# A buffer kept through the top-p steps: the mixing stage's first loads and its fold are moved into the end of the second step

## The reference

```python
# second layer, X = relu(norm(x))
for s in range(2):
    A = _adj_from_feats(Xa, W1, W2, W3)   # top-p softmax of Xa W1 W2 (Xa W3)^T
    Xf = R @ Xf
    Xa = A @ Xa
    Z = Z + (Xf @ U1s[s] + Xa @ U2s[s])
Y = X + Z
return (Y - mu) * rsqrt(var + LN_EPS) * gamma + beta
...
# third layer, 8 heads of 64
Wh = einsum('nf,hfd->hnd', x, W)
e_src = einsum('hnd,hd->hn', Wh, a1)
e_dst = einsum('hnd,hd->hn', Wh, a2)
```

## Time and profile before

| | |
|---|---|
| runs of the kernel | 3787.61, 3789.25, 3791.85 us |
| the profiled execution | 3794.3 us, span 3792.5 us |
| TensorE matmul, busy | 3378.6 us, 89% |
| VectorE, busy | 3207.5 us, 85% |
| ScalarE, busy | 2818.0 us, 74% |
| GpSimd, busy | 1394.7 us, 37% |
| DMA queue of SyncE (hardware) | 178.22 MB, 14.9% of 16 engines |
| second top-p step's last store | issued at 2320.5 us |
| mixing stage's first and last instruction | 2323.74 and 2486.6 us |

### The profile page before, as it was taken

One profiled execution on the slowest core, in us unless ns is written; L12 is line 12 of the kernel. 1 busy time (PEld: TensorE's weight loads), 2 busy tenths in 40 slices (PEclk: granted clock), 3 DMA queues, 4 the chain that ended last, 5 costly groups with the idle time before them and its releaser, 6 DMA issues. The chain is left out here.

```text
span 3792.5 us, 56639 instructions
## 1 busy us (share of the span) xinstructions
PE 3378.6 (89%) x20572; PEld 2050.0 (54%) x20628; DVE 3207.5 (85%) x5502; ACT 2818.0 (74%) x3508; POOL 1394.7 (37%) x1048
## 2 busy tenths in 40 slices
PE   7799999986969976899999965889999898999999
PEld 3699999743434433444444432368878443444444
DVE  3699999679999999599999996579998424999996
ACT  5699999559999999299999981267787334666664
POOL 0387444114545556146555661145553110000000
PEclk9999999998979988999999987999999999999999
DMA  6721110120111112311101004310000221111110
GB/s 235 270 79 31 36 31 25 57 67 26 53 37 36 46 44 97 117 47 45 34 20 28 25 17 130 147 26 21 21 21 10 74 77 67 48 48 55 51 50 17
DMA packets 166377, 224.46 MB, mean 59 GB/s; under 512 B 90466, under 2 KB 102720, under 8 KB 162976
## 3 DMA queue, kind: packets, MB, share of 16 engines
q1 hardware_dynamic: 147200, 178.22, 14.9%
q0 software_dynamic: 18896, 42.46, 3.5%
HBM read 148.36 MB, written 72.00 MB: 58 GB/s over the span
## 5 line engine op out<-in xcount | busy, mean ns | idle before, releaser
L1798 DVE SCALAR_TENSOR_TENSOR junk<-expd,mid 128x2048 bf16<-128x2048 f32 x440 | 1034.7, 2352 | 13.9
L604 ACT ACTIVATE steepz<-s1b,thr_h 128x512 bf16<-128x512 f32 (+1 forms) x928 | 774.3, 914 | 32.3 <-DVE A L675 20.3
L1694 ACT ACTIVATE junk_s<-expd,nmid 128x2048 bf16<-128x2048 f32 x250 | 498.5, 1994 | 3.8 <-POOL nmid L1736 3.4
L1698 ACT ACTIVATE junk_s<-junk_s 128x2048 bf16<-128x2048 bf16 x250 | 477.9, 1912 | 6.0
L758 PE MATMUL acc<-V,B 128*128 128x198 bf16 x4096 | 442.7, 251 | 35.3 <-DVE B L677 13.8
L765 PE MATMUL acc<-V,adjT 128*128 128x99 bf16 (+1 forms) x5248 | 415.5, 218 | 0.0
L1752 POOL TENSOR_SCALAR reach<-above,lack 128x1 f32<-128x1 f32 x202 | 231.5, 1146 | 457.8 <-ACT lack L1701 457.7
L1754 POOL TENSOR_SCALAR nmid<-reach,steps,nmid 128x1 f32<-128x1 f32 x202 | 377.5, 1869 | 21.2
L758 PEld LDWEIGHTS acc<-V,B 128*128 128x128 bf16 x4096 | 341.4, 98 | 38.6 <-issue 26.3
L765 PEld LDWEIGHTS acc<-V,adjT 128*128 128x128 bf16 x5248 | 340.4, 98 | 40.0 <-issue 0.3
L1553 PE MATMUL psX<-parts,block 128*128 128x512 bf16 x1482 | 339.1, 383 | 14.1 <-POOL ident L209 4.5
(11 more groups left out here) (319 smaller groups left out, 6230.5 us busy)
## 6 DMA issues: line engine op xcount, KB each, us to landing
rows<-in_adj_dram SPq DMA_DIRECT2D x16, 1024.0 KB, 8.7
s1b<-sT_dram SPq DMA_DIRECT2D x32, 512.0 KB, 3.7
block<-adj_dram SPq DMA_DIRECT2D x32, 512.0 KB, 4.4
plain_table<-rows POOLq DMA_DIRECT2D x16, 512.0 KB, 8.3
adj_dram<-adjT POOLq DMA_DIRECT2D x4, 2048.0 KB, 21.7
veil_table<-fill POOLq DMA_DIRECT2D x64, 128.0 KB, 2.5
y_dram<-yo SPq DMA_DIRECT2D x32, 256.0 KB, 2.0
adjT<-adj_dram SPq DMA_DIRECT2D x4, 2048.0 KB
```

Source lines behind the costliest of these rows:

```text
L604: act.activation(steepz[:, m % RELUS, :], s1b[:, q % 4, :], ACT.Relu, bias=thr_h[:, u, 1, j:j + 1], scale=STEEP).then_inc(relu_ready, 1)
L1694: act.activation(junk_s[:, u, :], expd[:, slot[i], :], ACT.Relu, bias=col(nmid, i), accum_out=col(above, i)).then_inc(sums_ready, 1)
L1698: act.activation(junk_s[:, u, :], junk_s[:, u, :], ACT.Sign, accum_out=col(over, i)).then_inc(sums_ready, 1)
L1798: link(dve.scalar_tensor_tensor(junk[:, :], e, col(mid, i), e, ALU.is_gt, ALU.mult, accum_out=found))
```

## The change

`adjT` is taken once, at the start of the program, and kept. While it holds no adjacency it serves as scratch: `xt`, `xo` and `rest` of `elu_project_stage`, and `expd`, `junk`, `junk_s` and `xo` of the top-p steps are views of it. So `parts` needn't be given back before the mixing stage, and the mixing stage's buffers `yt`, `xt`, `wp`, `gam`, `bet`, `avec` and `xo` are views of `parts` (class `Early`); its `w` is `w_out`, which held the keys `KT`. Since they exist in the step, a new letter `Z` in SyncE's string loads them there, once the last logits and the last `spread` are done: wp, avec, gam, bet, four tiles of xt, U2, and four tiles of yt. VectorE makes the eight pieces of the fold at the end of step 1. The mixing stage begins with tiles 4 and on, has no fold, and `BEHIND` is one less. The semaphores of the early loads belong to a scope of their own, which ends behind the mixing stage with one more clearing and barrier.

```diff
-         "giaagiyagiyaagiygiyagiyagiyagiyaagiyagiyagiyagiyagiygiygiygiyyxxxxx")},
+         "giaagiyagiyaagiygiyagiyagiyagiyaagiyagiyagiyagiyagiygiygiygiZyyxxxxx")},
...
+    def top_p_step(self, s, nat, tr, KT, w13n, parts, block16, xa_dram, xT_dram, kq_dram, parts_dram, y_dram,
+                   scratch, early, x_dram, w_dram, a1_dram, a2_dram):
...
-            expd = self.sb(st, "expd", [P, ROW_BLOCKS, N])
+            R = 2 * ROW_BLOCKS
+            expd = scratch[:, 0:R * N].bitcast(F32).rearrange("p (r n) -> p r n", r=ROW_BLOCKS)
+            junk = scratch[:, R * N:(R + 1) * N]
...
+                    elif c == "Z":
+                        sp.wait_ge(logits_ready, NT)
+                        sp.wait_ge(spread_ready, NT)
+                        for k in range(KD):
+                            sp.dma_start(early.wp[:, k, :].rearrange("p (h d) -> p h d", h=early.H),
+                                         w_dram[:, tile(k), :].rearrange("h p d -> p h d")).then_inc(early.wp_in, 16)
+                        for i, v in enumerate((a1_dram, a2_dram)):
+                            sp.dma_start(early.avec[:, i, :, :], v.partition_broadcast(P)).then_inc(early.a_in, 16)
+                        sp.dma_start(early.gam, a["L1_gnn_gamma"].partition_broadcast(P)).then_inc(early.g_in, 16)
+                        sp.dma_start(early.bet, a["L1_gnn_beta"].partition_broadcast(P)).then_inc(early.g_in, 16)
+                        for i in range(4):
+                            sp.dma_start(early.xt[:, i, :], x_dram[tile(i), :]).then_inc(early.x_in[i], 16)
+                        sp.dma_start(early.w[:, :, :], a["L1_gnn_U2_1"].rearrange("(k p) d -> p k d", p=P)
+                                     ).then_inc(early.w_in, 16)
+                        for i in range(4):
+                            assert rows.index(i) < n["y"]
+                            sp.wait_ge(y_out[0], 16 * (rows.index(i) + 1))
+                            sp.dma_start(early.yt[:, i, :], y_dram[tile(i), :]).then_inc(early.y_in[i], 16)
...
+                if s == 1:
+                    prod = junk[:, 0:2 * D].bitcast(F32).rearrange("p (h d) -> p h d", h=early.H)
+                    dve.wait_ge(early.wp_in, 16 * KD)
+                    dve.wait_ge(early.a_in, 32)
+                    for k in range(KD):
+                        for i in range(2):
+                            link(dve.tensor_tensor(prod, early.wp[:, k, :].rearrange("p (h d) -> p h d", h=early.H),
+                                                   early.avec[:, i, :, :], ALU.mult))
+                            link(dve.tensor_reduce(early.w12[:, k, i, :], prod, AX.X, ALU.add))
...
+    def mix_project_stage(self, nat, tr, early, nat_dram, y_dram, x_dram, x_new, adj_in, H, DH, g):
...
-            BEHIND = SOON + 4
+            BEHIND = SOON + 3
...
             def _(sp):
-                for t in range(2):
-                    sp.dma_start(yt[:, t, :], y_dram[tile(t), :]).then_inc(y_in[t], 16)
-                    sp.dma_start(xt[:, t, :], x_dram[tile(t), :]).then_inc(x_in[t], 16)
-                sp.dma_start(gam[:, :], a["L1_gnn_gamma"].partition_broadcast(P)).then_inc(g_in, 16)
-                sp.dma_start(bet[:, :], a["L1_gnn_beta"].partition_broadcast(P)).then_inc(g_in, 16)
                 for t in late:
                     sp.dma_start(nat[:, t, :], nat_dram[tile(t), :]).then_inc(nat_in, 16)
-                for k in range(KD):
-                    sp.dma_start(w[:, k, :], u2_dram[tile(k), :]).then_inc(w_in, 16)
-                for t in range(2, NT):
...
+                for t in range(4, NT):
+                    sp.wait_ge(o_read, t - 3)
+                    sp.dma_start(yt[:, t % 4, :], y_dram[tile(t), :]).then_inc(early.y_in[t % 4], 16)
+                    sp.wait_ge(x_ready, t - 3)
+                    sp.dma_start(xt[:, t % 4, :], x_dram[tile(t), :]).then_inc(early.x_in[t % 4], 16)
...
             def _(dve):
...
-                    if 6 <= t < 6 + 2 * KD:
-                        fold(t - 6)
...
+class Early:
...
+    def __init__(self, b, st, parts, w, w12, H, DH):
+        room = parts[:, :, :, :].rearrange("p t r d -> p (t r d)").bitcast(F32)
+        self.yt, self.xt = (room[:, 4 * n * D:4 * (n + 1) * D].rearrange("p (t d) -> p t d", t=4) for n in range(2))
+        self.wp = room[:, 8 * D:12 * D].rearrange("p (k d) -> p k d", k=KD)
...
```

More of the change, by code:

```diff
@@ L2535, in program @@
-            KT = w_out[:, :, :].rearrange("p k d -> p (k d)")
+            b.adjT = b.sb(sw, "adjT", [P, NT, N], BF16)
+            adj_in = b.sem(sw, "adj_in")
+            scratch = b.adjT[:, :, :].rearrange("p t n -> p (t n)")
+            with b.open() as sg:
+                g = Factors([b.sb(sg, name, [P, 16, n * NT])[:, :, :] for name, n in Factors.SIZES], sT_dram, top_dram)
+                b.project_stage(16, 32, a["x"], a["L0_gnn_W_seq"], a["L0_gnn_a1"], a["L0_gnn_a2"], natA, trB, g,
+                                a["adj"])
+                b.attention_stage(16, 32, 8, [1, 2, 3, 4, 5, 6, 7, 9, 10, 11, 12, 13, 14, 15], [], natA, B, g,
+                                  early=[(w_out[:, :, :], a["L0_gnn_W_out"].rearrange("(k p) d -> p k d", p=P))])
@@ new lines, in program @@
+                b.elu_project_stage(natA, trB, w_out, a["L0_gnn_b_out"], a["x"], xa, KT, parts, w13n, scratch)
+                b.top_p_stage(natB, trB, natA, trA, KT, w13n, parts, step_dram, xT_dram, kq_dram, parts_dram, y_dram,
+                              scratch, early, xa, a["L2_gnn_W"], a["L2_gnn_a1"], a["L2_gnn_a2"])
+                b.mix_project_stage(natB, trA, early, step_dram, y_dram, xa, xb, adj_in, 8, 64, g)
+            b.attention_stage(8, 64, 4, list(range(1, NT)), [1, 3, 5, 7, 9, 11, 13], natB, A, g, adj_in)
```

125 lines of the change are left out of this document (43 added, 82 removed).

## The result

The changed kernel takes 3771.94 us (median of 5 runs, 3763.87 to 3773.3) beside 3791.46 us before (5 runs, 3787.61 to 3795.61): ratio 0.9942, interval 0.9931 to 0.9953. The forecast was 3766 us with a range of 3757 to 3778 and faster. The profiled execution of the changed kernel took 3772.07 us (span 3770.3), 22.2 us less than that of before, where the sum of the prediction was 23.3.

A forecast was written before the change was run, and what follows sets the result against it. The edited stretch was taken as bound in turn by first loads, VectorE, both alternating, and TensorE. Gains 13.4 + 8.6 + 3.4 less 1.5 and 0.65 gave 23.3 us, so 3789.25 became 3766 us, range 3757 to 3778.

The forecast's parts named there:

- What bounds the kernel: End of second step and mixing stage: bound in turn by first loads, VectorE, VectorE and TensorE alternating, then TensorE.
- signs of a wrong forecast: Late look, looks over 5 us apart, TensorE idle staying near 13 us, or step growing by over 3 us.
- Z in SyncE's queue: Second step: Z ahead of yo's store delays ScalarE's copy 5.8 us; 1.5 us lost, ends 0 and 3.2.
- the store is later still: Rival, chance 0.12: Z moves at 220 GB/s, stall 7.1 us, net gain 17.7, total 3771 us.
- Part A: Mixing stage's start to TensorE's first turn: 38.5 us falls to 25.1, gain 13.4, ends 10.6 and 18.2.
- my sum without collisions: Mixing stage up to TensorE's first turn, if GpSimd's adds cost VectorE nothing: 20.3 us.
- VectorE keeps the pace: Rival, chance 0.17: in the mixing stage each GpSimd add costs VectorE its whole 1.27 us; gain 16.9, total 3772 us.
- Part B: Mixing stage, TensorE's first turn to first scores: 65.3 us falls to 56.7, gain 8.6, ends 0 and 13.1.
- part C: Mixing stage, first scores to the end: TensorE-bound and one sequence product shorter, gain 3.4 us.
- The extra barrier: Behind the mixing stage: clearing the new semaphores by themselves costs one more barrier, 0.65 us.

The follow-up runs named there:

- wp twice: Changed kernel with wp's four blocks loaded a second time, ahead of the rest of Z and the store of yo: 3779.69 us, ratio 0.9969.
- the fold in the stage: Changed kernel with the fold of the attention vectors put back into the mixing stage, its data still loaded early: 3778.36 us, ratio 0.9956.
- the store first: Changed kernel with Z issued behind the first of the step's last two stores of yo instead of ahead: 3768.30 us, ratio 0.9934.

## Why the prediction was right, and where it was off

**What bounds the kernel** held: each of the four phases moved as its bounding engine said, and the fold in the step's end costs nothing. VectorE's look stands 0.2 us behind the start, TensorE's first turn 23.9 us in, the first scores 80.9 and the next stage's start 137.9. One of my own signs of a wrong forecast did come, though: the step grew by over 3 us.

**Z in SyncE's queue** is the term that was mis-sized: 1.5 us put in, 4.79 measured, outside my bound of 3.2. It accounts for more than the whole difference between 23.25 and 21.17. The steps to it were mostly good: the rate of 260 GB/s (256 measured), the copy that waits, the slack of 2.6 us in VectorE. Two were not. The wait was 7.05 us instead of 5.8, since 260 GB/s was counted from Z's start with nothing for the store behind it. And the discount, that GpSimd's instructions shrink while VectorE stands still, did not hold to the end. It is true at the first decision: GpSimd's nmid ahead of it took 0.34 us instead of 2.45, and VectorE waited 3.14 us with ScalarE over 7 late, so that the decision itself was 5.6 us late. But ScalarE stays late, and the next decision is 6.9 us late again. It has hardly any idle time to give up (busy 38.0 of the 39.8 us from 2226.4 to 2266.2 in the kernel before), and this hand-over, 41 us on, asks for the rest: 1.37 + 0.19. Both hand-overs had about 2.6 us of slack before, and lateness less that slack, 7.05 - 2.6 = 4.45, would have been the better estimate. It is a lower bound and no more: over the six profiles with all of Z ahead of the store the step grew by 0.3 to 0.4 us more than it gives in four, by 0.9 with wp twice (10.67 beside 9.7) and by 1.6 with the fold in the stage (6.79 beside 5.2). How the stall divides between the hand-overs is not steady either: 3.14 and 1.37 in one profile of the changed kernel, 1.43 and 2.85 in the other.

The Trainium skill (DMA: Bandwidth & Descriptors, Queues, rings and completion order, on HWDGE ordering), which spoke against the place, is borne out: the store behind Z was late by the time of Z's bytes, and with the store ahead of Z the step lost nothing. Without that rule this term would have been 0, and wrong by all of the 4.8 us.

**The rival "the store is later still"** (17.7 us gained, 3771) has the mechanism that cost me the most, though its rate of 220 GB/s did not come and its stall of 7.1 was too large: the stretch gained 21.2 us, nearer to my 23.3. That its total of 3771 lies so near the measured 3771.94 is luck.

**Part A**: 14.63 against 13.4, right in kind. The 1.2 us too few are the adds: 0.42 us each for eight, 3.4 in all, instead of 0.8 for six, 4.8; with the adds cut to one column part A is 20.51 us, where my sum without collisions had 20.3. I had the place wrong, too: I charged xo and counted lines 141 and 152 as short. **The rival "VectorE keeps the pace"** falls with that, although its total, 3772, is the nearest of all. The Trainium skill (SBUF — State Buffer, SBUF: two separate sides, on the shared port pair) has a VectorE instruction that needs the pair and a GpSimd instruction exclude each other for the whole of it. The trace agrees: an xo of 1558 ns beside 752, and lines 141 and 152 that end with the add beside them. But what is paid is the rest of the add that is under way, and one add of 1.27 us cost 0.42 us on the average, since it often lies beside instructions that don't collide.

**Part B and part C**: 8.28 against 8.6, and 3.05 against 2.75. The terms of B's sum came as they stand: TensorE's work 51.0 us against 48.8 + 1.9, its three waits 4.44 against 4.5, the wait ahead of the scores 1.53 against 1.5. But 1.6 us of the gain are the clock behind the last wait, which the kernel before lost and this one kept; against the 59.36 us of the store first B would have gained 5.9, so a part of the agreement is luck. And what I put the gain down to was off. I gave all of B to the fold and 3.4 us in C to BEHIND. Undone singly, the fold is 4.6 us in B and BEHIND 4.1 in B and 3.4 in C, each with a share of the clock that equal kernels show too. That an instruction moved into a wait costs its place nothing, and spares the clock, was not in my reckoning; the product's 3.44 us in B I charged, and credited the same amount to waits that the fold alone would not have ended.

**The extra barrier**: 0.65 put in, 0.45 measured.

**The total**: 3766 was off by 6 us in the median. 2.2 of it are the kernel before, whose median moved from 3789.25 to 3791.46 with two more runs; 2.1 are the sum of the stretch, and the last 1.6 lie outside it, within what the runs of one kernel vary. The ratio puts the gain between 18 and 26 us of 3791, and the second measurement of the same kernel between 10 and 20.

## What to carry to other kernels

Before a pile of prefetches goes into a queue, look at what is queued behind it: a store whose buffer someone waits for belongs ahead of the pile, and moving one letter of the order bought back the 4.8 us that 5.24 MB of early loads had cost. Price such a stall as at least its lateness less the smallest slack at any later hand-over, with no discount for engines that get faster while the bound one stands still. And where two engines alternate, put ready work into the wait of the one that will be the bound next: the sequence product there cost nothing and spared 2.4 us of lower clock, while 8.5 us of products ahead of the wait made it 6.65 us long, and the lower clock behind it took back what they had gained.

## What the runs showed of the hardware

- In part B five waits of TensorE were between 3.96 and 6.65 us long, and each is followed by rows at the lower clock (4.69, 4.96 and 3.96 us: the next transposes 1.09 us instead of 0.63; 6.65 us: those, and a product of 6.15 us instead of 3.60; 4.13 us: transposes of 0.63 and a product of 5.30). Behind waits of 2.16 us it differs: in the changed kernel, twice, the transposes take 0.63 us and the product 3.60, in the kernel with the store first 1.02 and 4.94. Behind the first turn the first product takes 3.60 to 4.73 us. Both together are the 2.2 to 2.4 us between the changed kernel and the one with the store first, whose instructions in this part are the same.
- GpSimd's instructions on 128x1 numbers take 0.2 to 0.4 us where VectorE waits or is between two long instructions, and up to 2.5 us beside one (line 1775: 0.34 and 2.45 us). So in this chain of ScalarE, GpSimd and VectorE the hand-over came sooner while VectorE stood still.
- It goes the other way as well: VectorE's instructions of 0.17 us on 128x4 numbers (lines 141 and 152) took 1.0 and 1.2 us beside an add of GpSimd and ended within 0.05 us of it.
